# Attention in a transformer layer on eight cores: score tiles with the keys on the partitions, behind a separate pass for the row maxima

## The reference

```python
qg = q.reshape(B, S, NUM_KV_HEADS, GROUP, D)
scores = jnp.einsum('bqhgd,bkhd->bhgqk', qg, k) * scale
scores = jnp.where(causal[None, None, None, :, :], scores, jnp.asarray(-1e+30, dtype=scores.dtype))
probs = jax.nn.softmax(scores, axis=-1)
out = jnp.einsum('bhgqk,bkhd->bqhgd', probs, v)
```

## Time and profile before

| what | value |
|---|---|
| runs shown, median of 2 (lowest, highest) | 10186.52 us (10185.74, 10187.29) |
| the profiled execution's own time | 10013.21 us |
| its span, first to last instruction on the slowest core (core 2) | 10011.6 us |
| spans of the eight cores | 9961.2 to 10011.6 us |
| granted TensorE clock, mean of a core | 0.684 to 0.689 |
| PE busy over the span | 5150.6 us (51%) |
| DVE, ACT busy over the span | 2987.2 us (30%), 1846.9 us (18%) |
| attention, first scores to the last output DMA | 2375.6 to 6302 us |

### The profile page before, as it was taken

The page is one execution under the profiler, slowest core; times in us unless marked ns, Lnnn a source line. Parts: engine busy times, 40 slices in busy tenths (PEclk is TensorE's granted clock), DMA queues, the critical chain, the costliest instruction groups (busy, mean ns, idle before and its releaser), DMA issues.

```text
span 10011.6 us, 89374 instructions; the slowest of 8 cores (9961.2 to 10011.6 us)
## 1 busy us (share of the span) xinstructions
PE 5150.6 (51%) x26474; PEld 2622.2 (26%) x26944; DVE 2987.2 (30%) x4674; ACT 1846.9 (18%) x3801; POOL 248.4 (2%) x283
## 2 busy tenths in 40 slices
PE   1377777784334443333444444588851038888500
PEld 1133333332112222222233333243321013333200
DVE  3211111102333344444444444100014461000244
ACT  2100000001222222222233333000012221111111
POOL 0011111100000000000000000000000000000000
PEclk5688888896555555555555555799975559999755
DMA  2211111122000000000000000312222221221133
GB/s 85 69 38 38 38 38 38 38 56 81 9 24 6 7 22 4 4 4 4 4 4 3 4 4 3 106 43 50 50 66 105 118 93 32 48 48 41 68 147 134
DMA packets 118299, 444.42 MB, mean 44 GB/s; under 512 B 13521, under 2 KB 87377, under 8 KB 87889
## 3 DMA queue, kind: packets, MB, share of 16 engines
q0 software_dynamic: 16912, 119.74, 6.6%
q10 hardware_dynamic: 12962, 176.18, 4.5%
q1 hardware_dynamic: 87984, 142.74, 3.9%
HBM read 415.74 MB, written 142.61 MB: 56 GB/s over the span
## 4 chain that ended last, share of the span: by engine, by line
PE 45%; DVE 20%; DMA 12%; ACT 10%; issue 10%; another core or an unknown queue 1%; DVEq 1%; POOL 1%; ACTq 1%; POOLq 0%; SPq 0%
PE PB L344 5%; PE PA L344 5%; DVE stats L493 4%; PE PC L566 4%; DMA wq_sb<-wqkv 4%; ACT probs L502 3%; PE PB L816 3%; PE PA L816 3%; PE PB L654 3%; PE PA L654 3%; DVE stats L216 3%; PE PA L479 3%; DMA x_t<-xin 3%; DVE probs L547 3%; PE PC L344 2%
## 5 line engine op out<-in xcount | busy, mean ns | idle before, releaser
L566 PE MATMUL PC<-ident,probs 128*128 128x128 bf16 x2688 | 408.1, 299 | 2022.8 <-DVE probs L547 1871.5
L566 PEld LDWEIGHTS PC<-ident,probs 128*128 128x128 bf16 x2688 | 230.8, 124 | 2199.0 <-issue 2199.0
L29 DVE CAST probsT<-PC 128x512 bf16<-128x512 f32 (+3 forms) x768 | 479.8, 625 | 715.3 <-PE PC L566 645.9
L493 DVE TENSOR_REDUCE stats<-PA 128x1 f32<-128x1024 f32 (+4 forms) x384 | 401.9, 1047 | 502.4 <-PE PA L479 337.4
L344 PE MATMUL PB<-arena,wq_sb 128*128 128x512 bf16 x2006 | 474.4, 397 | 130.7 <-DMA wq_sb<-wqkv 128.1
L502 ACT ACTIVATE probs<-PA,stats 128x1024 bf16<-128x1024 f32 (+4 forms) x384 | 373.3, 972 | 884.1 <-DVE stats L493 651.9
L344 PE MATMUL PA<-arena,wq_sb 128*128 128x512 bf16 x2006 | 472.5, 395 | 114.5 <-DMA wq_sb<-wqkv 112.1
L28 ACT CAST probsT<-PD 128x512 bf16<-128x512 f32 (+3 forms) x512 | 259.0, 506 | 1208.2 <-PE PD L566 1208.2
L315 DVE TENSOR_TENSOR scr<-PE,sq_sb 128x512 f32<-128x512 f32 x64 | 44.0, 687 | 1148.9 <-PE PF L307 1148.9
L595 PE MATMUL PF<-probsT,vtm 128*128 128x128 bf16 x2304 | 285.5, 305 | 137.8 <-DVE probsT L29 75.5
L479 PE MATMUL PA<-k_sb,q_sb 128*128 128x512 bf16 (+2 forms) x576 | 286.8, 566 | 121.8 <-PE PC L566 27.9
(11 more groups left out here) (178 smaller groups left out, 6868.8 us busy)
## 6 DMA issues: line engine op xcount, KB each, us to landing
x_t<-xin ACTq DMA_DIRECT2D x32, 2048.0 KB, 9.2
wq_sb<-wqkv POOLq DMA_DIRECT2D x48, 1024.0 KB, 9.4
wslot<-wout POOLq DMA_DIRECT2D x32, 1024.0 KB, 17.2
x2s<-ln2tmp SPq DMA_DIRECT2D x16, 2048.0 KB, 6.3
wslot<-wffn POOLq DMA_DIRECT2D x32, 1024.0 KB, 16.5
x_t<-x2s ACTq DMA_DIRECT2D x16, 2048.0 KB
out<-y_t SPq DMA_DIRECT2D x16, 2048.0 KB, 9.8
Qs<-qout_sb SPq DMA_DIRECT2D x128, 128.0 KB, 7.3
```

The source lines that it names most:

```text
L29: return e.tensor_copy(d, s)
L493: vm = do("vector", lambda e, a=r["ap"], wd=wd, sb=sb: e.reduce_max(stats[:, sb:sb + 1], a[:, 0:wd], axis=AX.X, negate=True), inc="sV", wa ...
L566: do("tensor", lambda e, par=par, kc=kc, j=j, a=bk["ap"]: e.matmul(a[:, j * 128:(j + 1) * 128], probs[par][:, kc * 128:(kc + 1) * 128], id ...
```

## The change

Attention now works in two passes over a group, one head with 512 queries.

The first pass makes the same scores as before, without the mask (L488 of the new file), only for their row maxima: reduce (L498), minimum of the two halves (L505), copy to bf16 as a 128x1 column of `nmx_bf` (L509). TensorE transposes the column to 1x128 by a matmul with the identity (L512), into the upper columns of the region that the scores used, and ScalarE copies it to `nmxT_sb`.

The second pass, `mk_ph2`, loops over blocks of 128 keys. TensorE makes scores with the keys on the partitions and up to 512 queries along the row, in PC or PD (L538), adds the mask on diagonal blocks (L545) and adds the negated maxima by a matmul of one row of ones with `nmxT_sb` (L548). ScalarE makes the exponential into one of four `ptb` buffers (L557), which is already the operand that PV needs, so there are no transposes of probabilities and no copies of them. TensorE accumulates PV in PE2 (L567) and, by a matmul with a column of ones, the sums of the exponentials in one partition of PF (L573). At the end of the group VectorE takes the reciprocal of the 1x512 sums (L579), TensorE spreads it over the partitions by an fp32 matmul (L582), ScalarE copies it to SBUF, and VectorE multiplies PV by it (L592). The second pass of a group stands behind the first pass of the next group in every engine's list.

The mask is now also loaded in transposed form, and two tiles of ones are set at the start.

```diff
-    probs = [al(f"probs{i}", [128, 2048], BF16, offset=S0 + i * 4096) for i in range(4)]
-    probsT = [al(f"probsT{i}", [128, 2048], BF16, offset=S0 + 16384 + i * 4096)
-              for i in range(4)]
-    astg = [al(f"astg{i}", [128, 512], BF16, offset=S0 + 32768 + i * 1024) for i in range(2)]
+    ptb = [al(f"ptb{i}", [128, 512], BF16, offset=S0 + i * 1024) for i in range(4)]
+    astg = [al(f"astg{i}", [128, 512], BF16, offset=S0 + 4096 + i * 1024) for i in range(2)]
+    bcast_sb = [al(f"bcast_sb{i}", [128, 512], F32, offset=S0 + 6144 + i * 2048)
+                for i in range(2)]
+    nmxT_sb = [al(f"nmxT_sb{i}", [1, 512], BF16, offset=S0 + 10240 + i * 1024)
+               for i in range(2)]
+    recT_sb = [al(f"recT_sb{i}", [1, 512], F32, offset=S0 + 12288 + i * 2048)
+               for i in range(2)]
+    nmx_bf = al("nmx_bf", [128, 8], BF16, offset=S0 + 16384)
...
-                        if diag:
-                            do("tensor", lambda e, a=r["ap"], o=qt * 128 - off: e.matmul(
-                                a[:, o:o + 128], ident[:, :], mask_sb[:, :],
-                                start=False, stop=True),
...
-                        vm = do("vector", lambda e, a=r["ap"], wd=wd, sb=sb: e.reduce_max(
-                            stats[:, sb:sb + 1], a[:, 0:wd], axis=AX.X, negate=True),
-                            inc="sV", waits=vw)
...
-                    vr = do("vector", lambda e, par=par, sb=sb: e.tensor_scalar_mul(
-                        probs[par][:, 0:1024], probs[par][:, 0:1024],
-                        stats[:, sb + 4:sb + 5]), inc="sV",
-                        waits=(("sA", af1), ("sA", rfree[0])))
...
-                vnorm = do("vector", lambda e, par=par, sb=sb, W=W: e.tensor_scalar_mul(
-                    probs[par][:, 0:W], probs[par][:, 0:W], stats[:, sb + 5:sb + 6]),
-                    inc="sV", waits=(("sV", vrec),))
...
-                        do("tensor", lambda e, par=par, kc=kc, j=j, a=bk["ap"]: e.matmul(
-                            a[:, j * 128:(j + 1) * 128],
-                            probs[par][:, kc * 128:(kc + 1) * 128],
-                            ident[:, :], start=True, stop=True),
-                           inc="sT" if j == cg - 1 else None, waits=wts)
...
-                        do("tensor", lambda e, kc=kc, H=H, par=par, a=pb["ap"]: e.matmul(
-                            a[:, 0:128],
-                            vtm[:, kc * 1024 + H * 128: kc * 1024 + (H + 1) * 128],
-                            probsT[par][:, kc * 128:(kc + 1) * 128],
-                            start=(kc == 0), stop=(kc == nkc - 1)),
...
+                    vm = do("vector", lambda e, a=r["ap"], wd=wd, cix=cix, nh=len(vparts):
+                            e.reduce_max(stats[:, cix + nh:cix + nh + 1], a[:, 0:wd],
+                                         axis=AX.X, negate=True),
+                            inc="sV", waits=(("sT", pe_sc),))
+                    vparts.append((cix + len(vparts), vm))
+                    r["free_v"] = vm
+                if len(vparts) == 2:
+                    vm = do("vector", lambda e, c0=vparts[0][0], c1=vparts[1][0]:
+                            e.tensor_tensor(stats[:, c0:c0 + 1], stats[:, c0:c0 + 1],
+                                            stats[:, c1:c1 + 1], op=ALU.min),
+                            inc="sV", waits=(("sV", vparts[1][1]),))
+                c0 = vparts[0][0]
+                vc = do("vector", lambda e, c0=c0, gp=gp, qtl=qtl: e.tensor_copy(
+                    nmx_bf[:, gp * 4 + qtl:gp * 4 + qtl + 1], stats[:, c0:c0 + 1]),
+                    inc="sV", waits=(("sV", vm),))
+                do("tensor", lambda e, a=lastr["ap"], gp=gp, qtl=qtl: e.matmul(
+                    a[0:1, 896:1024],
+                    nmx_bf[:, gp * 4 + qtl:gp * 4 + qtl + 1], ident[:, :],
+                    start=True, stop=True),
+                   inc="sT", waits=(("sV", vc), ("sT", nmxT_used[gp])))
+                pe_tr = cnt("sT")
+                ev = do("scalar", lambda e, a=lastr["ap"], gp=gp, qtl=qtl: CP(
+                    e, nmxT_sb[gp][0:1, qtl * 128:(qtl + 1) * 128], a[0:1, 896:1024]),
+                    inc="sA", waits=(("sT", pe_tr),))
+                lastr["free_a"] = ev
+                nmx_evs.append(ev)
+            nmx_ready = nmx_evs[-1]
+
...
+            def mk_ph2(tb=tb, hg=hg, H=H, gp=gp, sp=sp, qp=qp, nmx_ready=nmx_ready):
+                nkc = tb * 4 + 4
+                last_exp = 0
+                for kc in range(nkc):
+                    j0 = max(0, kc - tb * 4)
+                    cw = 512 - j0 * 128
+                    diag = kc >= tb * 4
+                    bk = stbank[kc % 2]
+                    pb = kc % NPB
+                    wts = (("sA", nmx_ready), ("sV", CONSTV))
+                    if bk["exp"]:
+                        wts = wts + (("sA", bk["exp"]),)
+                    do("tensor", lambda e, kc=kc, j0=j0, cw=cw, H=H, hg=hg, qp=qp,
+                       a=bk["ap"]: e.matmul(
+                           a[:, j0 * 128: j0 * 128 + cw],
+                           k_sb[:, H * S + kc * 128: H * S + (kc + 1) * 128],
+                           q_sb[qp][:, hg * 512 + j0 * 128: hg * 512 + 512],
+                           start=True, stop=False),
+                       inc=None, waits=wts)
+                    if diag:
+                        do("tensor", lambda e, j0=j0, a=bk["ap"]: e.matmul(
+                            a[:, j0 * 128:(j0 + 1) * 128], ident[:, :], maskT_sb[:, :],
+                            start=False, stop=False), inc=None)
+                    do("tensor", lambda e, j0=j0, cw=cw, gp=gp, a=bk["ap"]: e.matmul(
+                        a[:, j0 * 128: j0 * 128 + cw], ones_bf[0:1, 0:128],
+                        nmxT_sb[gp][0:1, j0 * 128: 512],
+                        start=False, stop=True), inc="sT")
+                    pe_st = cnt("sT")
+                    wex = (("sT", pe_st),)
+                    if pbuf_user[pb]:
+                        wex = wex + (("sT", pbuf_user[pb]),)
+                    last_exp = do("scalar", lambda e, pb=pb, j0=j0, cw=cw, a=bk["ap"]:
+                                  e.activation(ptb[pb][:, j0 * 128: j0 * 128 + cw],
+                                               a[:, j0 * 128: j0 * 128 + cw], AF.Exp,
+                                               bias=0.0, scale=1.0),
+                                  inc="sA", waits=wex)
+                    bk["exp"] = last_exp
+                    wpv = (("sA", last_exp),)
+                    if kc == 0:
+                        wpv = wpv + (("sV", pv_free0[0]), ("sA", bc_last[0]),
+                                     ("sV", CONSTV))
+                    do("tensor", lambda e, kc=kc, H=H, pb=pb, j0=j0, cw=cw, nkc=nkc:
+                       e.matmul(PE2[:, j0 * 128: j0 * 128 + cw],
+                                vtm[:, kc * 1024 + H * 128: kc * 1024 + (H + 1) * 128],
+                                ptb[pb][:, j0 * 128: j0 * 128 + cw],
+                                start=(kc == 0), stop=(kc == nkc - 1)),
+                       inc=None, waits=wpv)
+                    do("tensor", lambda e, kc=kc, pb=pb, j0=j0, cw=cw, nkc=nkc:
+                       e.matmul(PF[0:1, j0 * 128: j0 * 128 + cw], ones_bf1[:, 0:1],
+                                ptb[pb][:, j0 * 128: j0 * 128 + cw],
+                                start=(kc == 0), stop=(kc == nkc - 1)),
+                       inc="sT")
+                    pbuf_user[pb] = cnt("sT")
+                pe_grp = cnt("sT")
+                vrc = do("vector", lambda e, gp=gp: e.reciprocal(
+                    recT_sb[gp][0:1, :], PF[0:1, 0:512]), inc="sV",
+                    waits=(("sT", pe_grp),))
+                do("tensor", lambda e, gp=gp: e.matmul(
+                    PF[:, 0:512], ones_f[:, :], recT_sb[gp][0:1, :],
+                    start=True, stop=True), inc="sT", waits=(("sV", vrc),))
+                pe_bc = cnt("sT")
+                bc = do("scalar", lambda e, gp=gp: CP(e, bcast_sb[gp][:, :], PF[:, 0:512]),
+                        inc="sA", waits=(("sT", pe_bc), ("sV", bcast_used[gp])))
+                bc_last[0] = bc
+                wev = (("sA", bc),)
+                if aspill[sp]:
+                    wev = wev + (("sQA%d" % sp, aspill[sp]),)
+                ve = do("vector", lambda e, sp=sp, gp=gp: e.tensor_mul(
+                    astg[sp][:, :], PE2[:, 0:512], bcast_sb[gp][:, :]),
+                    inc="sV", waits=wev)
+                pv_free0[0] = ve
+                bcast_used[gp] = ve
+                do("sync", lambda e, sp=sp, hg=hg, tb=tb: e.dma_start(
+                    out=As[:, hg * S + tb * 512: hg * S + (tb + 1) * 512],
+                    in_=astg[sp][:, :]),
+                   inc="sQA%d" % sp, n=16, waits=(("sV", ve),))
+                aspill[sp] += 16
+                nmxT_used[gp] = pe_grp
+
+            if pend_ph2[0] is not None:
+                pend_ph2[0]()
```

(7 more changed lines are left out.)

163 lines of the change are left out of this document (32 added, 131 removed).

## The result

| what | before | after |
|---|---|---|
| median (lowest, highest), runs of both taken together | 10085.7 us (10006.97, 10205.4), 10 runs | 12329.05 us (12259.36, 12494.54), 11 runs |
| the profiled execution's own time | 10013.21 us | 12348.59 us |
| attention section of the profiled core | 3926.4 us | 6216.1 us |
| cores: span, mean granted clock | 9961.2 to 10011.6 us, 0.684 to 0.689 | 12234.3 to 12347.0 us, 0.633 to 0.645 |

The changed kernel is slower: the ratio is 1.2277, with a 95% interval of 1.2242 to 1.2312. In some executions of every kernel here one or both halves of the chip show a lower granted clock and the time is 1 to 5% longer; ratios and intervals leave these executions out, the medians in this document do not. The forecast was 12345 us.

The account below looks back on a forecast made before the run. The attention section (3926 us) was held bound by a chain of engine hand-overs, no engine full. Its rebuilt terms, 3394 + 1857 + 722 + 112 = 6085 us, add 2159 to the 10186.5 us median: 12345 us, range 11,700 to 12,800.

Parts of the forecast that it names:

- part 1: Second pass over the keys: closed loop of 2.89 us per full step, 3394 us together.
- entering: Start of each group's second pass: satisfied waits estimated at 0.4 us per group, 51 us.
- part 2: First pass (maxima): per query block, scores, VectorE maxima and a column transpose ahead of the next scores; 1857 us.
- the product's delay: Group's end: VectorE's product delays the next group's first maximum by 0.61 to 1.35 us; 112 us.
- part 3: End of a group: one-partition reciprocal 3.25 us, then fp32 broadcast, with TensorE waiting; 5.64 us x128 = 722 us.
- C: Group's end: the reciprocal streams in 0.69 us; -328 us, 12,017 us in all; chance 15%.
- D: Group's end: the divide takes eight cycles an element, 4.4 us; +147 us, 12,492 us in all; chance 15%.
- The clock: Attention section: granted clock expected at 0.50 (1.2 GHz), with 59% streaming, short waits and idle TensorE at group ends.
- Rival A: Clock rises to 2.4 GHz in the second pass and stays; saves 1243 us, 11,102 us in all; chance 6%.
- Rival B: Second pass: TensorE takes next block's scores while PV waits, at 2.4 GHz; -566 us, 9620 us; chance 3%.
- 1.2 GHz case: Attention section with next scores taken while PV waits, clock not risen: 4603 us, +677, 10,863 us in all.
- full-clock case: Attention section with next scores taken while PV waits, at 2.4 GHz: 3360 us, 956 of it second pass.

Follow-up runs that it names:

- e1: Changed kernel with scores and exponential of the next key block issued ahead of PV and row sum: 11281.81 us, ratio 1.1056 to the kernel before.
- e3: Changed kernel with 128x128 ones for the row sum and a zero-padded 128-row bias matmul: 12072.02 us, ratio 1.1882 to the kernel before.
- e5: Changed kernel with a group's four maxima transposes together behind the previous group's second pass, one copy: 11475.34 us, ratio 1.1252 to the kernel before.
- e10: Changed kernel with next block's scores ahead of PV and a 128-row bias matmul, row sum still one column: 10330.55 us, ratio 1.0299 to the kernel before.
- e7: Changed kernel with next block's scores ahead of PV, 128x128 ones for the row sum and a 128-row bias matmul: 10333.72 us, no interval.

## Why the prediction was right, and where it was off

- **The direction and the closed loop (part 1).** Right. The wait that is shown is the one foretold: 1107.4 us in front of PV, 0.89 us a step (about 1.0 was forecast). e1 takes the loop away and gives 1134 us back.
- **The step's length (part 1).** 3.06 us instead of 2.89, just outside the 2.8 to 3.0 that was named as the sign of being right; second pass 3589 instead of 3394 (with entering). The term that was mis-sized is the spacing of matmuls: 3 x 0.427 and 0.64 were taken, from rows where loads are covered; it was 0.51, 0.52, 0.54 and 0.60 to the hand-over. Against it, ScalarE to PV took 0.14 us (5403.93 + 0.60 to 5404.67), not 0.24, which was read from an fp32 broadcast. e3 isolates the load: 0.30 us of a step.
- **The first pass (part 2) and the product's delay.** 1857 + 112 = 1969 forecast, 1880 measured. The mechanism is right: e5, which takes the transposes out from between the blocks, takes more than half of it away. The size was 89 us too large, and 42 of these are the way from a group's last transpose to its second pass: the forecast had 0.69 us there and then 0.4 more for entering, and it is 0.35 (43.2 us in the 124 groups where the one follows the other). The 0.69 itself was put down to satisfied waits. Between the blocks it came out at 0.67, but in e5 the score matmuls start 0.26 us behind the last transpose with the same list of waits, so what makes it up stays open.
- **The group's end (part 3).** 722 forecast, 494 + 252 = 746 measured. The reciprocal was put at 3.25 us between bounds of 0.69 and 5.8, and is 3.35. Rivals C and D were both off. The Trainium skill ("VectorE: DVE Perf Modes", section "First, the fixed hardware budget") has a repeat count of 8, which led to the estimate of 4.4 us. The runs don't agree: (3346 less 160) / 512 is 6.2 ns an element, for 1 and for 128 partitions. The 5 ns above a streamed element, which the forecast took from 164 against 159 ns in the earlier trace rows, came near. With bounds of 0.69 and 5.8 us around it, that was partly luck.
- **The clock.** 0.50 came true, but the reason was only part of it. It was put down to short waits and idle ends; e1 has no wait in the second pass and stays at 0.50, and e3 has full shapes and stays too. The new order with 128 rows in the bias matmul reaches 0.65 (e10), with the full row sum besides 0.66 (e7). That the clock before rose only behind work without a gap was misread: in the forecast's own last row the QKV projection has 0.88 with TensorE busy 1376.41 of 1800 us. Rival A is dead for this order.
- **Rival B.** Its order doesn't come about by itself: TensorE stood in front of L567 with the next scores behind. Made by hand (e1), it gives a section of 5082 us, near the 4603 of its 1.2 GHz case once the uncovered loads are added (0.42 us by 1280 steps at most, 538 us), and far from the 3360 of its full-clock case. Even with full shapes (e7) the second pass is 1409 us, not 956.
- **The sum.** The section is 6216 us against 6085 forecast, 2% more: 195 us too little in the second pass, 89 too much in the first, 24 too little at the group's end. That the median comes out 0.1% from the forecast is luck. From median to median the time grew by 2243 us, 84 more than forecast, but from 10085.7 us, 101 under the 10186.5 on which the forecast was put. Put on the profiled execution, from which the sum was made, the forecast was 12172 us, and the profiled execution of the changed kernel took 12348.59, 1.4% more.

## What to carry to other kernels

Count the engine hand-overs in one turn of a loop and look at what stands ahead of each wait in the waiting engine's list; buffers for the next turn are worth nothing while its work stands behind the wait. Removing instructions (89374 before, 80757 after) saved nothing by itself here. Order, shapes and the end of the group, changed in what was left, took over 3,600 us from a section of 6,216. On TensorE a small operand isn't a cheap one: give weights and moving operand their full 128 rows and columns where zeros or repeated ones do no harm.
